# Summing each block's edges in one burst of quarter-width matmuls, with a ring of 22 gathered tiles

## The reference

```python
x = x + gnn(layernorm(x))          # see below
x = x + ffn(layernorm(x))          # silu(x Wg) * (x Wu), then Wd; weights ternary by groups of 128

deg   = segment_sum(ones, dst)
agg   = segment_sum(x[src], dst)            # the edge sums
h     = x @ W_self + b + (agg / max(deg, 1)) @ W_neigh
h     = layernorm(h) * gamma + beta
h     = where(h >= 0, h, alpha * h)
return h + x
```

## Time and profile before

| | us |
|---|---|
| median of 2 runs | 1696.73 |
| lowest, highest | 1694.02, 1699.44 |
| span of the profiled execution | 1674.1 |

### The profile page before, as it was taken

The page is one execution under the profiler, slowest core; times in us unless marked ns, Lnnn a source line. Parts: engine busy times, 40 slices in busy tenths (PEclk is TensorE's granted clock), DMA queues, the critical chain, the costliest instruction groups (busy, mean ns, idle before and its releaser), DMA issues.

```text
span 1674.1 us, 21796 instructions
## 1 busy us (share of the span) xinstructions
PE 1537.9 (92%) x6421; PEld 750.7 (45%) x6422; DVE 1055.9 (63%) x2305; ACT 1177.1 (70%) x2248; POOL 938.3 (56%) x936
## 2 busy tenths in 40 slices
PE   7999989987889999999999998999998998989897
PEld 3444434444444454444444444444444443444343
DVE  8999624655565565564665756557466466573876
ACT  5577500026777787778787786869887887879796
POOL 2123277666676666666666766667666666764000
PEclk9999989989998999999999999999999999999999
DMA  9869488997776887777777867787777777784101
GB/s 303 257 219 292 125 293 313 274 282 208 213 226 189 225 224 221 218 229 210 216 212 226 228 201 230 209 235 211 217 209 223 218 213 223 206 228 129 38 14 37
DMA packets 210883, 353.40 MB, mean 211 GB/s; under 512 B 105482, under 2 KB 105482, under 8 KB 210754
## 3 DMA queue, kind: packets, MB, share of 16 engines
q0 software_dynamic: 70560, 231.27, 47.4%
q1 hardware_dynamic: 140204, 120.73, 24.5%
HBM read 295.79 MB, written 39.62 MB: 200 GB/s over the span
## 4 chain that ended last, share of the span: by engine, by line
PE 84%; issue 6%; ACT 6%; DVE 2%; DMA 1%; another core or an unknown queue 0%; DVEq 0%; SPq 0%; ACTq 0%
PE f_ps L994 21%; PE f_ps L995 20%; PE f_ps L807 20%; PE agg_ps L889 10%; PE agg_ps L891 10%; ACT f_ps L1088 4%; PE side_ps L934 1%; PE agg_ps L803 1%; PE side_ps L803 1%; PE f_ps L889 0%; PE f_ps L891 0%; ACT hT L1113 0%; ACT acc L1098 0%; DVE acc L1440 0%; DMA rows<-in_x 0%
## 5 line engine op out<-in xcount | busy, mean ns | idle before, releaser
L759 POOL DMA_INDIRECT rows<-node_table,idx x882 | 891.6, 1011 | 442.6 <-issue 241.3
L1088 ACT ACTIVATE f_ps<-f_ps,ratio 128x512 f32<-128x512 f32 (+2 forms) x1303 | 777.0, 666 | 240.6 <-PE f_ps L995 163.2
L994 PE MATMUL f_ps<-x1T,tern 128*128 128x512 f16 (+2 forms) x1144 | 424.2, 374 | 52.0 <-issue 28.2
L995 PE MATMUL f_ps<-x1T,tern 128*128 128x512 f16 (+2 forms) x1144 | 422.4, 372 | 0.0
L889 PE MATMUL agg_ps<-rows,hot 128*128 128x512 f16 x846 | 328.5, 388 | 22.8 <-issue 22.8
L891 PE MATMUL agg_ps<-rows,hot 128*128 128x512 f16 x846 | 326.1, 385 | 4.3 <-issue 4.3
L1440 DVE SCALAR_TENSOR_TENSOR acc<-f_ps,scl,acc 128x512 f32<-128x512 f32 (+2 forms) x143 | 102.4, 717 | 229.0 <-PE f_ps L995 116.4
L994 PE MATMUL f_ps<-hT,tern 128*128 128x512 f16 (+2 forms) x572 | 213.4, 376 | 25.6 <-issue 13.0
L995 PE MATMUL f_ps<-hT,tern 128*128 128x512 f16 (+2 forms) x572 | 212.6, 374 | 0.0
L994 PEld LDWEIGHTS f_ps<-x1T,tern 128*128 128x128 f16 x1144 | 113.1, 99 | 216.6 <-issue 67.2
L889 PEld LDWEIGHTS agg_ps<-rows,hot 128*128 128x128 f16 x846 | 120.1, 142 | 133.3 <-issue 64.2
(11 more groups left out here) (176 smaller groups left out, 1705.1 us busy)
## 6 DMA issues: line engine op xcount, KB each, us to landing
rows<-node_table,idx POOLq DMA_INDIRECT x882
hsx<-own_rows SPq DMA_DIRECT2D x49, 256.0 KB
hsx<-in_x SPq DMA_DIRECT2D x48, 256.0 KB
out_nodes<-work SPq DMA_DIRECT2D x48, 256.0 KB, 2.2
xj<-xnt_rows SPq DMA_DIRECT2D x26, 256.0 KB
node_table<-work SPq DMA_DIRECT2D x25, 256.0 KB, 3.1
acc<-own_rows SPq DMA_DIRECT2D x23, 256.0 KB
own_rows<-acc SPq DMA_DIRECT2D x23, 256.0 KB
```

Of the source, the lines that this page charges most:

```text
L759: pool.indirect_dma_start(out=rows[:, j, :], out_offset=None, in_=table[:, :], in_offset=bass.IndirectOffsetOnAxis(ap=of[:, j:j + 1], axis ...
L994: pe.matmul(to, lhs, parts[0], start=g == 0, stop=False, skip_group_check=True)
L995: pe.matmul(to, lhs, parts[1], start=False, stop=True, skip_group_check=True).then_inc(p_ff, 1)
L1088: act.activation(ps, ps, ACT.Copy, scale=ratio[:, w if up else 2, j:j + 1]).then_inc(a_scaled, 1)
```

## The change

1. **Edge layout.** A tile is now 128 consecutive edges (before, tile `j` held every eighteenth edge). Since the edges are sorted, the 32 nodes of a quarter of a block have their edges in a few neighbouring tiles. Quarter `q` takes tiles `4q - 1` to `4q + 5`: 7 rounds, one tile per quarter in each.
2. **The sums.** `sum_block` replaces `sum_step`. It stands after the last tick of the slot, and holds 54 matmuls of 32 columns, four quarters side by side in four groups of 32 columns and output partitions. `p_used` is raised after rounds 2, 4 and 6.
3. **The ring.** `rows` has 22 places instead of 18, so the gathers can be four tiles ahead of the block in use.
4. **Edge lists.** They are loaded as 18 rows of 512 bytes, turned on TensorE in fp32 (`turn_edges`, tick 6), and copied out of PSUM by VectorE (`take_edges`, tick 9), one slot earlier than before.
5. **One-hot and degrees.** `hot` has 8 x 128 columns instead of 18 x 128. One reduction replaces three.
6. **Ranges.** VectorE's passes over 2450 elements are gone. GpSimd compares (`count_segments`, 9800 elements, two passes), TensorE counts with 50 + 5 matmuls after block 23 of the prologue, and VectorE does small operations on the result. A flag marks blocks whose quarters do not fit their windows, or edges not in order; those go through the slow path `overflow`. With these inputs no block is marked, and none went that way before.
7. **Planner.** `PACE, EVEN` go from 38, 35 to 42, 39; `turn_out` may stand at ticks 2, 7 and 12. One buffer of the table's stores is dropped (`YR` 6 to 5), as is one bank of the prologue's products (`YB` 6 to 5).

```diff
-    PACE, EVEN = 38.0, 35.0
+    PACE, EVEN = 42.0, 39.0
...
-    AGG_AT = [[] for _ in range(TICKS)]
-    for j in range(STEPS):
-        AGG_AT[2 + j * (TICKS - 2) // STEPS].append(j)
+    def tile_of(q, i):
+        return QUARTERS * q - 1 + i
...
+    FREE_AFTER = (2, 4, 6)
...
-        rows = sb("rows", [P, STEPS, 2 * D], F16)
+        rows = sb("rows", [P, RING, 2 * D], F16)
...
-                for load in range(LOADS):
-
-                    after(pool, p_used, (b - 1) * LOADS + load + 1 if b else 0)
-                    gather_load(idx[:, b % 2], load, gathered[load])
+                for j in range(STEPS):
+                    g = b * STEPS + j
+                    if g % 2 == 0 and g >= RING:
+                        pool.wait_ge(p_used, used_count((g - RING) // 2))
+                    gather(g % RING, idx[:, b % 4, j:j + 1], gathered[g % RING // 2])
...
+            def turn_edges(b):
+                pe.wait_ge(ld_edges[b % 2], 32 * (b // 2 + 1))
+                if b == 2:
+                    pe.wait_ge(v_inv, 1)
+                if b > 2:
+
+                    pe.wait_ge(v_h0, b - 2)
+                pe.transpose(edge_bank(b), edges[:, b % 2, :], identf[:, :]).then_inc(p_edges, 1)
...
+                if i == RANGES_FROM + 14:
+                    pe.wait_ge(pool_counts, 1)
+                    for n in range(NSEG):
+                        pe.matmul(first_ps[:, 0:NQ], onesm[0:EP, :], hit[:, n, :], start=(n == 0), stop=(n == NSEG - 1))
...
+            def sum_block(b):
+                pe.wait_ge(v_hot, b + 1)
+
+                pe.wait_ge(v_inv, b + 1)
+                pe.wait_ge(v_idx, 2 * min(b + 3, BLOCKS))
+                waited = 0
+                for i in range(WINDOW):
+                    of_round = [q for q in range(QUARTERS) if tile_of(q, i) >= 0]
+                    pairs = max(tile_of(q, i) for q in of_round) // 2 + 1
+                    for n in range(waited, pairs):
+                        pair = b * PAIRS + n
+                        pe.wait_ge(gathered[pair % (RING // 2)], 32 * (pair // (RING // 2) + 1))
+                    waited = pairs
+                    for part in range(2):
+                        for q in of_round:
+                            lo = q * QN
+                            mm = pe.matmul(agg_ps[lo:lo + QN, :], hot[:, b % 2, i, lo:lo + QN],
+                                           rows[:, (b * STEPS + tile_of(q, i)) % RING, part * D:(part + 1) * D],
+                                           start=(part == 0 and i == (0 if q else 1)),
+                                           stop=(part == 1 and i == WINDOW - 1), skip_group_check=True)
+                    if i in FREE_AFTER:
+                        mm.then_inc(p_used, 1)
...
+                if t < BLOCKS:
+                    sum_block(t)
...
+            def one_hot(b):
...
+                dve.tensor_tensor(by_quarter(hot[:, b % 2]), windows(b), by_quarter(node_j[:, None, :].broadcast_to((P, WSLOTS, P))), ALU.is_equal).then_inc(v_hot, 1)
...
+                    dve.tensor_reduce(degs[:, :], hot[:, b % 2].rearrange("p i m -> p m i"), AX.X, ALU.add).then_inc(v_degs, 1)
```

More of the change, by code:

```diff
@@ L23 @@
 STEPS = 18
-PER_LOAD = 2
-LOADS = STEPS // PER_LOAD
+PAIRS = STEPS // 2
+RING = 22
+QUARTERS, QN = 4, 32
+WINDOW, WSLOTS = 7, 8
+OSTEPS = 8
 TICKS = 18
-BIG = float(1 << 17)
+BIG = 1 << 14
+NO_NODE = -20000.0
 FAR = 20000.0
@@ L592, in overflow @@
                             end = sp.value_load(rangei[0:1, bass.ds(b + BLOCKS, 1)], min_val=0, max_val=E)
-                            with sp.Fori(first, end, PASS) as at:
+                            with sp.Fori(first, end, OPASS) as at:
                                 n = sp.snap(passes)
@@ L755, in _, with gather @@
                 pool.wait_ge(st_xt[i], 16 * len(range(i, len(LATER), XTR)))
-            def gather_load(of, load, s):
-                for j in range(load * PER_LOAD, (load + 1) * PER_LOAD):
-                    pool.indirect_dma_start(
-                        out=rows[:, j, :], out_offset=None, in_=table[:, :],
-                        in_offset=bass.IndirectOffsetOnAxis(ap=of[:, j:j + 1], axis=0)).then_inc(s, 16)
+            def gather(at, of, s):
+                pool.indirect_dma_start(
+                    out=rows[:, at, :], out_offset=None, in_=table[:, :],
+                    in_offset=bass.IndirectOffsetOnAxis(ap=of, axis=0)).then_inc(s, 16)
             def overflow():
@@ L776, in overflow @@
                                 pool.sem_inc(pool_turn, 1)
-                                for load in range(LOADS):
-                                    gather_load(idx_o, load, o_rows)
+                                for j in range(OSTEPS):
+                                    gather(j, idx_o[:, j:j + 1], o_rows)
                                 pool.reg_add(passes, passes, 1)
@@ L823, in _ @@
                     turn0(1)
+                if i == RANGES_FROM + 14:
+                    pe.wait_ge(pool_counts, 1)
+                    for n in range(NSEG):
+                        pe.matmul(first_ps[:, 0:NQ], onesm[0:EP, :], hit[:, n, :], start=(n == 0), stop=(n == NSEG - 1))
+                    for n in range(5):
+                        mm = pe.matmul(first_ps[:, 2 * P:2 * P + EROW // 5], onesm[0:EP, :],
+                                       unordered[:, n * EROW // 5:(n + 1) * EROW // 5], start=(n == 0), stop=(n == 4))
+                    mm.then_inc(p_counts, 1)
+                if i == BLOCKS - 3:
+                    pe.wait_ge(v_rngi, 1)
+                    turn_edges(0)
+                    turn_edges(1)
             def overflow():
@@ L871, in degree @@
             def degree(b):
[L872 to L894 removed]
+                pe.wait_ge(v_degs, b + 1)
@@ new lines, in degree @@
+                after(pe, v_h0, b)
+                pe.matmul(agg_ps[:, 0:1], degs[:, :], ones[:, 0:1], start=True, stop=True).then_inc(p_deg, 1)
+            def sum_block(b):
[3 more added lines that the diff above has]
+                waited = 0
+                for i in range(WINDOW):
+                    of_round = [q for q in range(QUARTERS) if tile_of(q, i) >= 0]
[13 more added lines that the diff above has]
+                        mm.then_inc(p_used, 1)
@@ L1300, in count_edges @@
                 after(dve, p_deg, b)
-                for lo, hi in ((0, 44), (44, 88), (88, P)):
-                    with nc.allow_low_precision(reason="whole numbers up to STEPS"):
-                        dve.tensor_reduce(degs[:, lo:hi], hot[:, b % 2, lo:hi, :], AX.X, ALU.add).then_inc(v_degs, 1)
-                    yield
+                with nc.allow_low_precision(reason="whole numbers up to WSLOTS"):
+                    dve.tensor_reduce(degs[:, :], hot[:, b % 2].rearrange("p i m -> p m i"), AX.X, ALU.add).then_inc(v_degs, 1)
             for b in range(2):
```

362 lines of the change are left out of this document (188 added, 174 removed).

## The result

The changed kernel takes 2283.79 us (two runs, 2283.58 and 2284.0) against 1696.73 us: 1.346 times as long, 95% interval 1.341 to 1.352. I had predicted 1587 us. Most of this document is about one number behind that: the same two kernels, run again on another occasion (one execution each), took 1590.2 and 1520.7 us.

A forecast was written before the change was run, and what follows sets the result against it. TensorE was taken as the bound (23.9 of 27.2 us per slot), GpSimd 0.3 us behind. Slots -106, early slots -4, block 0 -5, prologue +7, tail -2 gave -110: 1564 us span, 1587 us; range 1530 to 1665.

The forecast's parts named there:

- Gathers: GpSimd's 18 gathers per slot: four tiles ahead cover landing with 0.4 us left, so GpSimd runs without a stop.
- my sum: Whole kernel: slots -106, early slots -4, block 0 -5, prologue +7, tail -2, together -110 us.
- My own signs of being wrong: In the trace: sum rows one by one, GpSimd idle 3 us per slot, first gather over 15 us later, clock under 0.95.
- Rival 2: Gathers to sums: the ring starves TensorE, about 3 us lost per slot, slot 26.5 us, 1662 to 1700 us; chance 0.18.
- What bounds the kernel now: Slot of 27.2 us before the change: TensorE first with 23.9 us of work, GpSimd 23.6, ScalarE 21.7.
- Slot: Time per block of 128 nodes: 27.2 us falls to 24.8 us, between 23.3 and 26.5.
- ScalarE's share of 85 to 90%: Sign of being right: ScalarE busy 85 to 90% of the slot, from 80% before.
- Burst: Edge sums on TensorE: 54 quarter matmuls mostly side by side, 4 us per slot instead of 7.8.
- Rival 1: Edge sums on TensorE: the quarters do not run side by side, burst 11.7 us, about 1800 us; chance 0.12.
- Planner, VectorE: Slots: same 132 steps per four slots, bunched more; VectorE's work falls about 1.8 us, reduction 1.2, compare 0.6 to 1.1.
- Prologue: Ahead of the slots: counting matmuls and GpSimd passes add 7 us, between 0 and 15.
- The offset: Whole kernel: the median of the runs stays 22.6 us above the profiled span.

The follow-up runs named there:

- e12: The kernel before with a small GpSimd fill and wait after every pair of gathers, run a second time: 1595.2 us, beside a kernel before of 1520.7 us.
- e8: The kernel before with a small GpSimd fill and wait after every pair of gathers, first run: 1593.6 us, beside a kernel before of 1525.4 us.
- e11: The changed kernel itself, unedited, run again on another occasion: 1590.2 us, beside a kernel before of 1520.7 us.
- e5: The changed kernel with GpSimd's two prologue passes over 9800 elements cut into ten parts each: 2239.4 us, beside a kernel before of 1703.2 us.
- e4: The changed kernel with each indexed gather replaced by a plain transfer of 128 consecutive table rows: 1553.6 us, beside a kernel before of 1525.4 us.
- e15: The kernel before itself, unedited, run again for its own trace: 1699.7 us, beside a kernel before of 1696.4 us.
- e18: Repeat of e4, the changed kernel with plain transfers in place of indexed gathers: 1554.7 us, beside a kernel before of 1520.1 us.
- e1: The changed kernel with GpSimd waiting for ScalarE's count ahead of each pair of gathers from block 6: 1837.5 us, beside a kernel before of 1703.2 us.
- e13: The changed kernel with GpSimd's passes cut in ten and gather pairs paced by ScalarE's count from block 6: 1623.0 us, beside a kernel before of 1520.7 us.

## Why the prediction was wrong

**The step that failed is in "The change part by part", *Gathers*:** "So GpSimd can run without a stop". I counted that as a gain. The wait ahead of each pair was priced as nothing but lost GpSimd time, and what its removal would do to the other engines wasn't asked. On the occasion of the prediction's own pair, GpSimd issuing gathers in runs of 18 is what costs: a slot of 24.8 us forecast, 39.3 measured. From the first norm to the last my sum has 1197 us (1307 less 106 and 4), measured were 1884: 687 us of a miss of 697. (The first norm came 28 us later than forecast and the tail was 3 us longer; an offset that was 21 us smaller made up for most of that.) My own signs of being wrong came: GpSimd idle with the sums as releaser, a first gather over 15 us later, a mean clock under 0.95 (0.80). None of my rivals held it. Rival 2 was nearest (GpSimd idle with the sums as releaser), but it put 3 us on a slot where there are 16 (785 / 49), and its cause, too little cover by four tiles, is not the cause.

**The bound was misread, in "What bounds the kernel now".** TensorE's work was 23.9 us of a slot of 27.2, and the remaining 3.3 us I left unexplained, carried forward as slack. Part of them were in the profile as idle time with no visible releaser, such as GpSimd's 67.4 us with the releaser "remote". On free occasion D the kernel before spans 1518.3 us. With the 238.7 us of e12 ahead of the first norm and its 121.3 us behind the last, that leaves 24.1 us a slot, an estimate (24.2 by e8 on occasion B): TensorE's 23.9 with next to nothing over. So about 3 of the 27.2 us belong to the held occasion. The late counts in the trace of before (22%) are the one difference that I can name for them; that they are all of it is not shown. This change could not remove them, and I promised 2.4.

**On a free occasion most terms come out, and the sign still doesn't.** There the changed kernel takes 1590.2 us against 1520.7, 1.046 times as long; that this is near my 1587 is chance, since its reference is another. Point by point, with e11:
- *Slot*: 24.8 forecast, 24.8 measured. But the slot of before is 24.1 there, so it grew. ScalarE's share of 85 to 90%: 88% (265 of 300 us, from 850 to 1150).
- *Burst*: 4 us forecast, 3.2 measured. Rival 1 is out. 54 matmuls on the same rows took 14 x 0.22 + 0.2 us. The Trainium skill's rule ("TensorE: Matmul & The Clock Gate", Part 3: Packing small matmuls) that weight loads overlap only when the row groups differ, which spoke against the change, did not show in the time.
- *Planner, VectorE*: the slots go from 20.5 to 29.5 us, in which I read the planner's bunching; no run has the old planner's pace. The reduction takes 1.91 us, not 1.2; the compare 1.22, just above my 0.6 to 1.1. Harmless to VectorE's load (190 of the same 300 us), but in e11 the burst waits 37 us in all for the compare and 18 us for the degree ratio.
- *Prologue*: +7 forecast, between 0 and +15. Measured +32 (first gather 240.9 against 208.8 us), the same on either kind of occasion. GpSimd's two passes lasted 16.7 and 25.0 us, where I had 22 and 11 to 22; together they are inside the 33 to 44 of the two. The step that failed is "in the 40 us or so in which it had nothing to do": I asked whether GpSimd had the time and not whom its passes would hold up. With the passes cut (e5) the first gather comes at 220.6 us, and the 11.8 us that are left lie inside the range.
- *Where the 70 us lie on occasion D* (spans of 1588.4 and 1518.3 us): +35 ahead of the first norm, +33 in the 48 slots, +1.5 in the tail. Since the slot of before is what is left of its span, this adds up by construction and proves nothing. The 3.7 us per slot taken from TensorE bought nothing. With GpSimd nearly unloaded the slot is still 24.0 us (e4), so GpSimd makes up 0.8 us of it; that ScalarE with its bunched steps makes up the rest fits its 272 of 300 us, but is argued, not tested.

**The offset.** I kept 22.6 us between the profiled span and the median as if it were overhead. It is 1.8 us in after and 2.5 us in e15. The first profiled execution, 1674.1 us, was a shorter one than the two that were timed; held occasions vary too, from 1671.8 to 1703.2 us for this kernel.

**What stays open**: what the condition is. All kernels of an occasion agree on its kind. Occasions B and E bear the same chip number and are of different kinds, so that number doesn't tell it. Whether recording has a part in it is untested. I also can't say whether indexed gathers are needed for it (e18 missed), or whether matmuls end late or only their counts.

## What to carry to other kernels

A wait that paces one engine can be what keeps the others going: before taking it away, look at what the engines do in those stretches of the old trace where it happens to be absent, and explain idle time without a releaser before counting on it. Compare the number of semaphore records with the number due: here a shortfall marked every trace of a held occasion. Keep long GpSimd passes over SBUF in pieces when VectorE has small operations that a chain hangs on. And run the kernel before beside every experiment, since here it moved by 12% from one occasion to another and a change of 1.35 became one of 1.05.

## What the runs showed of the hardware

- On some occasions, while GpSimd issues gathers 1.25 us apart, TensorE's completions reach ScalarE, VectorE and GpSimd late (30% of them by over 0.5 us in after, the latest by 13.9 us) and, in the stretch shown, come in a bundle when the last gather has landed; on others the same program shows none of it (e11). VectorE's and ScalarE's recorded completions are never late. The price was 694 us for the changed kernel (2283.8 against 1590.2) and 176 us for the kernel before (1696.7 against 1520.7).
- On such occasions TensorE at times stops inside a round of matmuls, where the program has no wait: 76 stops of over 0.5 us in e1, none in e13 on a free one.
- On such occasions a trace has 66 to 87% of the semaphore counts due, on free ones over 99.7%.
- A VectorE operation on 7 elements lasted 23.91 us beside a GpSimd pass of 24.97 us.
- Column tiles: 54 matmuls of 32 columns, 512 elements each, in 3.2 us, near the 14 x 0.22 us of 14 half rounds of four.
- A sum over 8 strided fp16 values (1024 elements per partition) took 1.91 us on VectorE, where 792 contiguous ones took 0.94.
